# A fused attention and FFN layer: its first stage ordered by one list of all parts, and 30 weight pieces in place of 42 measured in the context's buffer

## The chip, the cores and the metric

The kernel runs on one core of a Trainium2 chip. Its time is the device time of one execution in microseconds (us), the median of several runs. Beside it stands one profiled execution, from which all rows are taken.

## The reference

The input x is (2, 512, 1024). The layer computes

```
n = layernorm(x)
x = x + xattn(n, positions, context)      # context: (2, 1024, 256), used as the weights of a gated MLP
m = layernorm(x)
W = base + mean(|w - base|) * sign(w - base)      # for each of w1, w2, w3 (3584 x 1024)
x = x + (silu(m @ W1.T) * (m @ W3.T)) @ W2.T
```

`xattn` reads the 1024 channels as 256 heads of 4 ways (a small product per head and a normalization), makes q, k and v, turns them by position, takes a causal softmax of 16 heads for each of the 2 batches, and writes the result back into the 1024 channels by a gated update with softplus and exp factors. Then it reads the channels again (two outputs), multiplies them with the context's two matrices, takes silu(gate) * up, and writes back by a second update of the same kind. All is in float32.

For the FFN the mean of |w - base| over a whole matrix must be known before the first weight is used. So each matrix is read once to be measured, 128 rows at a time ("pieces": 28 for each matrix, 84 in all), and later again to be used.

## The kernel before

The work is cut into 8 tiles of 128 rows, 4 for each batch. It has two stages.

The **first stage** does the cross-attention layer and, beside it, the measuring of w1 and w3 (pieces 0 to 55; `SOON` is 56). Its parts have names (stage, number, part):

- `front` (tile, 17 parts): normalization, transposes, the small products with `diag` (the mask product, part 6), q, k and v, their transposes.
- `fill`, `use`, `weigh` (48 units; `fill 36` is unit 36): scores by TensorE into four PSUM banks, then either the maximum (VectorE) or the exponential (ScalarE) as `use`, then the product with v. `turnmax` and `out` belong to groups of units. Units 0 to 24 belong to batch 0, the rest to batch 1 but for unit 23, which begins batch 1. The four banks of scores are shared, so each fill waits for the use of the unit before.
- `row` and `back` (tile): the first write-back, and the read for the MLP. `back` part 20 writes `inT`, the MLP's input.
- `mlp` (32 blocks, 8 for each half batch): 8 matmuls with the context's matrices in `ctxw`, silu, a product.
- `finish` (tile): second write-back, statistics of the new rows.
- `norm` and `turn` (4 tiles each): normalization and transposes for the FFN, in upper and lower parts.
- `measure` (56 pieces): the SP queue loads a piece and its base (512 KB each), VectorE takes the difference (GpSimd for every third piece), ScalarE the absolute sum (`me_abs` counts the pieces done).
- `ctx`: the 2 MB load of the context's matrices into `ctxw`. `coef`: the coefficients from the sums (two small steps of VectorE around a matmul of TensorE). `raw`, `prep`, `upper`, `blend`: the first four weight rows of the FFN, made ready. `early`: the first products of the FFN.

Pieces are measured in buffers that stand in turn (`PARTS` is 3). Pieces whose number is a multiple of 3 use `part`. The two others use `ctxw` as long as their number is below `LATER`, and from then on `big[0]`, the buffer of batch 0's q and k. So `ctx` waits until `LATER` pieces are measured, and the load of piece `LATER` waits for the last weighing of batch 0:

```python
if t == LATER:
    sp.wait_ge(at_pv, TURN[last_unit("T", len(GROUPS) // 2 - 1)] + 1)
```

`phase_one_order()` makes the order of the parts on each engine (TensorE is "PE", VectorE "DVE", ScalarE "ACT", GpSimd "POOL") when the program is built. It goes through time with estimated durations. Of the parts that are ready it takes the one with the lowest `start - LEAD[...]`, the start less a tabulated lead. The engines then work through their lists in this order and wait for each other by semaphores; the durations of the plan have no other effect.

`LULLS` names parts of TensorE ahead of which it multiplies a unit matrix some times (line 1449): "filler". An entry is (count, bank, the user whose readers are waited for first, or None for half-width filler with no wait). It keeps TensorE active where the plan expects a wait.

The **second stage**, `ffn_order()`, has its own lists: the products with w1 and w3, then those with w2. The diff leaves it alone.

Of the kernel before, what the change touches and what calls it, by code (L numbers as in the profile page):

```python
# [152 lines left out]
LATER, SOON = 42, 2 * JT  # L153
# [232 lines left out]
def lead(key):  # L386

    stage, t, part = key
    return LEAD[stage, part][t]


def phase_one_order():
# [58 lines left out]
    while ready:  # L451
        best = None
        for key in sorted(ready):
# [12 lines left out]
            rank = start - lead(key)  # L466
# [50 lines left out]
LEAD = {  # L517
    ("back", 0): (-225.99, -238.77, -359.66, -358.29, -450.97, -468.31, -612.22, -231.01),
    ("back", 1): (6.37, -89.84, -35.64, -348.36, -186, -305.43, -474.36, -667.36),
    ("back", 2): (-228.52, -249.15, -129.37, -360.12, -325.24, -303.49, -528.41, -614.89),  # L520
    ("back", 3): (205.51, -257.89, -88.79, -223.09, -268.08, -203.44, -510.34, -530.38),
    ("back", 4): (-218.43, -230.15, -178.8, -145.66, -451.83, 66.43, -631.77, -586.7),
    ("back", 5): (-223.08, -263.97, -355.17, -282.96, -403.66, -382.05, -485.87, -605.69),
    ("back", 6): (59.69, -290.89, -357.39, -385.03, -474.02, -448.04, -675.86, -616.52),
    ("back", 7): (-236.06, -225.1, -389.92, -48.43, -486.21, -474.98, -393.21, -602.33),
    ("back", 8): (3.19, 30.32, -358.28, -216.22, -486.97, 67.58, -576.98, -587.55),
    ("back", 9): (-281.25, -230.88, -180.3, -381.58, -482.31, -357.42, -625.94, -537.35),
    ("back", 10): (-137.74, -303.66, -410.08, -427.11, -515.73, -517.64, -49.04, -698.31),
    ("back", 11): (-44.49, -119.5, -276.51, -375.63, -232.23, -539.45, -686.78, -416.34),
    ("back", 12): (-301.88, -360.67, -52.9, -232.33, -409.01, -548.28, -591.09, -246.37),  # L530
    ("back", 13): (-43.29, -323.83, -467.45, -499.71, -556.47, -654.5, -112.56, -766.07),
    ("back", 14): (-328.52, -191.13, -479.38, -228.06, -630.23, -354.83, -709.43, -448.81),
    ("back", 15): (5.12, 84.02, -501.87, -542.37, -260.17, -556.77, -826.53, -818.8),
    ("back", 16): (51.96, -375.05, -217.05, -528.19, -473.77, -546.52, -618.88, -737.93),
    ("back", 17): (-338.82, -410.57, -498.3, -444.63, -593.01, -373.83, -463.09, -566.26),
    ("back", 18): (-239.72, -98.17, -407.24, -521.88, -643.69, -697.12, -475.37, -298.36),
    ("back", 19): (-385.54, -423.62, -538.78, -598.71, -633.12, -505.57, -834, -837),
    ("back", 20): (-389.19, -441.08, -439.18, -198.64, -742.05, -462.03, -517.88, -801.02),
    ("blend", 0): (-1059.06, -1156.9),
    ("blend", 1): (-959.72, -721.92),  # L540
    ("blend", 2): (-875.88, -814.02),
    ("blend", 3): (-526.23, -1037.71),
    ("coef", 0): (-305.16,),
    ("coef", 1): (-615.23,),
    ("coef", 2): (-468.02,),
    ("ctx", 0): (-101.35,),
    ("diag", 0): (-56.53, -68.11),
    ("dump", 0): (-636.99, -735.49, -753.18, -747.54, -823.09, -101.99, -907.87, -1049.67),
    ("early", 0): (-922.69, -879.16),
    ("early", 1): (-576.9, -1205.82),  # L550
    ("early", 2): (-720.49, -1030.56),
    ("early", 3): (-1112.76, -1458.21),
    ("fill", 0): (53.95, -90.28, 282.32, -156.82, 31.83, 16.1, -177.4, -184.3, -194.93, -204.96, 50.55, -224.38, -235.42,
# [3 lines left out]
    ("finish", 0): (-283.94, -582.73, -661.89, -707.35, -834.71, -847.17, -919.46, -594.69),  # L557
    ("finish", 1): (-564.04, -588.05, -697.69, -724.73, -714.26, -492.51, -751.68, -914.48),
    ("finish", 2): (-522.27, -519.79, -506.87, -269.19, -632.11, -627.22, -704.37, -832.85),
    ("finish", 3): (-519.56, -488.19, -146.36, -805.7, -639.26, -746.76, -682.15, -891.98),  # L560
    ("finish", 4): (-136.2, -619.53, -610.47, -722.85, -834.27, -876.3, -938.57, -777.13),
    ("finish", 5): (-581.47, -630.04, -454.56, -619.34, -694.69, -863.44, -377.22, -909.27),
    ("finish", 6): (-90.19, 155.1, -723.98, -828.01, -406.89, -492.71, -888.55, -603.59),
    ("finish", 7): (-642.57, -617.83, -431.62, -680.22, -605.76, -793.54, -935.11, -973.45),
    ("finish", 8): (-587.11, -463.8, -503.4, -540.37, -233.96, -647.05, -885.61, -816.41),
    ("finish", 9): (-586.05, -412.71, -574.27, -450.54, -756.17, -793.11, -673.91, -655.59),
    ("finish", 10): (-297.89, -587.86, -639.11, -572.34, -851.43, -626.67, -764.65, -818.29),
    ("finish", 11): (-655.12, -522.12, -778.09, -509.5, -309.29, -806.88, -962.53, -807.86),
    ("finish", 12): (-385.93, -591.05, -838.04, -760.91, -676.85, -649.05, -414.26, -805.06),
    ("finish", 13): (-179.73, -658.06, -841.99, -465.23, -629.34, -894.12, -975.43, -969.75),  # L570
    ("finish", 14): (-721.85, -465.58, -844.37, -477.77, -887.04, -517.18, -874, -766.54),
    ("finish", 15): (-737.68, -743.87, -875.66, -861.7, -859.57, -745.65, -977.29, -781.37),
    ("finish", 16): (-753.16, -293.46, -694.49, -473.82, -935.94, -650.63, -748.65, -538.42),
    ("front", 0): (340.88, -61.51, 92.28, 91.21, -69.31, -82.02, 247.14, -185.56),
    ("front", 1): (182.29, -23, 21.77, -47.12, 162.48, 97.92, -71.75, -68.38),
    ("front", 2): (112.65, -19.03, 290.76, 118.66, 74.76, -86.16, -172.38, -215.67),
    ("front", 3): (-77.36, 18.8, 118.95, -60.39, 356.01, 276.47, 50.59, -254.36),
    ("front", 4): (188.4, 310.84, 55.13, 148.26, 106.28, -11.75, -176.25, 36.87),
    ("front", 5): (481.18, 247.19, 74.37, 76.9, 118.23, 402.54, -4.28, -260.56),
    ("front", 6): (117.35, -67.3, -14.78, 18.98, 162.28, 283.35, -193.47, -293.39),  # L580
    ("front", 7): (88.36, 5.08, 66.5, 63.87, -89.59, -156.74, 214.83, -282.62),
    ("front", 8): (26.63, -68.61, 39.51, 18.86, -84.64, 15.93, -213.04, 94.99),
    ("front", 9): (101.49, 120.16, 261.78, 153.29, -38.03, 89.3, -29.56, -292.97),
    ("front", 10): (624.51, -68.67, -83.91, -81.82, 451.18, -164.66, -34.07, -7.36),
# [2139 lines left out]
```

## Time and profile before

| | us |
|---|---|
| median of 3 runs | 1232.62 (1226.36 to 1236.79) |
| profiled execution, its own time | 1234.41 |
| its span, first to last instruction | 1232.6 |
| TensorE busy | 1181.4 (96%) |
| VectorE busy | 939.4 (76%) |
| ScalarE busy | 703.1 (57%) |
| GpSimd busy | 353.9 (29%) |
| mean granted clock of TensorE | 0.989 |

Read it as shares over two stages that differ: busy times by stretch are what tells them apart. TensorE's busy time holds the filler too. The granted clock is a share of 2.4 GHz; a stretch with 0.75 was half of its time at 1.2 GHz.

### The profile page before, as it was taken

The numbers are of one execution on the slowest core, as the hardware profiler recorded it, in microseconds if no ns is written. First come the engines' busy times: TensorE is split into PE (matmuls) and PEld (weight loads), VectorE is DVE, ScalarE is ACT, GpSimd is POOL, SyncE is SP. The second block draws the span as 40 slices with busy tenths as digits, with TensorE's granted clock in tenths as the row PEclk, the third lists the DMA queues.
The fourth block names the chain that finished last, engine by engine and source line by source line (L and its number), as shares of the span: only waits on it lengthen the run. The fifth ranks groups of instructions, "written<-read, shape, count | busy, mean of one in ns | idle before, by whom it ended". The sixth has DMA issues, their size and how long they took to land. (4 is left out here: it accounts for less than half of the span.)

```text
span 1232.6 us, 17284 instructions
## 1 busy us (share of the span) xinstructions
PE 1181.4 (96%) x6276; PEld 920.6 (75%) x6276; DVE 939.4 (76%) x1279; ACT 703.1 (57%) x1007; POOL 353.9 (29%) x441
## 2 busy tenths in 40 slices
PE   7988889999997999999999999999999999999998
PEld 4765554656775888878888888888788888888887
DVE  6778778778878867787777977778775777888864
ACT  4878667575557666557565666656655333334342
POOL 2233333423522334243553344433340000000000
PEclk8999899999999999999999999999999999999999
DMA  8366678865021257767687676776776968753232
GB/s 353 124 248 246 242 259 303 328 224 199 19 86 51 87 165 254 241 189 242 219 278 237 201 229 211 259 240 189 213 237 222 337 243 277 252 205 120 101 125 99
DMA packets 99065, 257.37 MB, mean 209 GB/s; under 512 B 9363, under 2 KB 23973, under 8 KB 98469
## 3 DMA queue, kind: packets, MB, share of 16 engines
q1 hardware_dynamic: 94948, 241.59, 54.6%
q0 software_dynamic: 4032, 14.68, 6.7%
q8 instruction: 50, 0.82, 0.3%
q14 instruction: 35, 0.28, 0.1%
HBM read 214.81 MB, written 41.42 MB: 208 GB/s over the span
## 5 line engine op out<-in xcount | busy, mean ns | idle before, releaser
L2585 POOL TENSOR_TENSOR raw_w<-raw_w,raw_base 128x256 f32<-128x256 f32 x224 | 197.2, 924 | 184.5 <-DMA raw_base<-in_mean_w 184.3
L2129 ACT ACTIVATE split<-grid 128x1024 fp32r<-128x1024 f32 x98 | 104.0, 1061 | 160.7 <-PE pair L1653 147.7
L2527 DVE TENSOR_TENSOR split<-grid,split 128x1024 fp32r<-128x1024 f32 x98 | 119.7, 1225 | 61.8 <-ACT split L2129 61.6
L1653 PE MATMUL quad<-split 128*128 128x512 f32 x588 | 149.3, 389 | 0.5 <-DVE hid L2534 0.5
L1653 PE MATMUL pair<-split 128*128 128x512 f32 x588 | 149.2, 389 | 0.0
L1653 PEld LDWEIGHTS quad<-split 128*128 128x128 f32 x588 | 110.4, 188 | 23.6 <-DVE split L2527 0.9
L1653 PEld LDWEIGHTS pair<-split 128*128 128x128 f32 x588 | 110.5, 188 | 22.8
L2308 DVE TENSOR_TENSOR ring_lo<-raw_base,ring_hi 128x1024 fp32r<-128x1024 f32 x56 | 70.0, 1251 | 33.1 <-ACT ring_hi L2074 27.1
L1606 PE MATMUL pair<-t_b_hi,ring_hi 128*128 128x512 f32 x224 | 89.0, 397 | 2.8 <-ACT snap L2093 2.7
L1606 PE MATMUL pair<-xnT_hi,ring_hi 128*128 128x512 f32 x224 | 87.4, 390 | 0.7 <-ACT t_b_lo L1981 0.7
L1606 PE MATMUL pair<-t_b_lo,ring_hi 128*128 128x512 f32 x224 | 87.8, 392 | 0.0
L1606 PE MATMUL pair<-xnT_lo,ring_hi 128*128 128x512 f32 x224 | 87.3, 390 | 0.0
L1606 PE MATMUL pair<-xnT_hi,ring_lo 128*128 128x512 f32 x224 | 87.2, 389 | 0.0
L1606 PE MATMUL pair<-t_b_hi,ring_lo 128*128 128x512 f32 x224 | 87.2, 389 | 0.0
L2304 DVE SCALAR_TENSOR_TENSOR raw_w<-quad,coeff,raw_base 128x1024 f32<-128x1024 f32 x52 | 66.5, 1280 | 19.6 <-ACT quad L1923 19.3
L2308 DVE TENSOR_TENSOR ring_lo<-raw_w,ring_hi 128x1024 fp32r<-128x1024 f32 x28 | 40.4, 1445 | 46.1 <-ACT ring_hi L1932 46.1
L1923 ACT ACTIVATE quad<-raw_w 128x1024 f32<-128x1024 f32 x52 | 53.1, 1022 | 26.7 <-POOL raw_w L2585 26.1
L2585 POOL TENSOR_TENSOR ctxw<-ctxw 128x256 f32<-128x256 f32 x56 | 44.1, 817 | 69.8 <-DMA ctxw<-in_mean_w 69.8
L2647 POOL DMA_DIRECT2D late<-in_w x28 | 24.9, 891 | 126.0 <-ACT late L2105 126.0
L2216 DVE TENSOR_REDUCE negwide<-quad 128x4 f32<-128x512 f32 (+3 forms) x32 | 46.9, 1488 | 13.2 <-PE quad L1543 13.1
L1606 PEld LDWEIGHTS pair<-t_b_hi,ring_hi 128*128 128x128 f32 x224 | 42.2, 188 | 13.4 <-ACT snap L2093 5.0
L1864 ACT ACTIVATE prob<-quad 128x1536 f32<-128x1536 f32 (+1 forms) x24 | 38.2, 1590 | 21.2 <-PE quad L1555 12.8
(338 smaller groups left out, 2759.6 us busy)
## 6 DMA issues: line engine op xcount, KB each, us to landing
raw_w<-in_w SPq DMA_DIRECT2D x56, 512.0 KB, 5.7
raw_base<-in_mean_w SPq DMA_DIRECT2D x56, 512.0 KB, 7.4
grid<-h_blocks SPq DMA_DIRECT2D x49, 512.0 KB, 3.7
ctxw<-in_w SPq DMA_DIRECT2D x28, 512.0 KB, 4.3
ctxw<-in_mean_w SPq DMA_DIRECT2D x28, 512.0 KB, 5.7
late<-in_mean_w SPq DMA_DIRECT2D x28, 512.0 KB, 7.5
late<-in_w POOLq DMA_DIRECT2D x28, 512.0 KB, 6.1
grid<-in_mean_w SPq DMA_DIRECT2D x28, 512.0 KB, 4.7
```

The source lines that it names most:

```text
L1606: a = pe.matmul(bank, ww[:, at + k, :], xx, start=first and k == 0 and n == 0, stop=k == half - 1 and n == 2, skip_group_check=not first)
L1653: a = pe.matmul(into[t], found[:, a, t * P:(t + 1) * P], found[:, b, :], start=p == 0 and n == 0 and q < 4, stop=p == PAIRS - 1 and n == 2 ...
L1864: act.activation(probs[TURN[u] % 2][:, :, 0:cols], quad[:, :, 0:cols], ACT.Exp).then_inc(at_p, 1)
L1923: act.activation(spare.rearrange("p a b -> p (a b)"), w[:, :], ACT.Sign).then_inc(f_sign, 1)
L2129: act.activation(splits[n % RINGS][:, 0:2, :], operands(n), ACT.Copy).then_inc(a_hi, 1)
L2216: a = dve.tensor_reduce(found.rearrange("p r j -> p (r j)"), quad[:, :, at:at + cols], AX.X, ALU.max, negate=True)
L2304: dve.scalar_tensor_tensor(w[:, :], sign, coeff[:, k:k + 1], base[:, :], ALU.mult, ALU.add).then_inc(f_w, 1)
L2308: dve.tensor_tensor(whole_of(pair[1]), source, whole_of(pair[0]).bitcast(F32), ALU.subtract).then_inc(done, 1)
L2527: dve.tensor_tensor(found[:, 2:4, :], operands(n), found[:, 0:2, :].bitcast(F32), ALU.subtract).then_inc(a_lo, 1)
L2585: a = pool.tensor_tensor(w[:, some], w[:, some], base[:, some], ALU.subtract)
L2647: pool.dma_start(lates[n % LATES][:, :], d["w2"][n], accum_op=ALU.add).then_inc(ld_add[n % LATES], 16)
```

## The change

The plan's rule is replaced. `LEAD` and `lead(key)` go. A table `RANK` takes their place: each of the 1014 parts has a place of its own, 0 to 1013, and of the ready parts the one with the lowest place is taken. The table came from a search. `LATER` goes from 42 to 30. The `LULLS` table is made anew for the new order. Nothing else is changed.

```diff
-LATER, SOON = 42, 2 * JT
+LATER, SOON = 30, 2 * JT
...
-def lead(key):
-
-    stage, t, part = key
-    return LEAD[stage, part][t]
...
-            rank = start - lead(key)
+            rank = RANK[stage, part][t]
...
-    ("ctx", 0): (-101.35,),
-    ("front", 0): (340.88, -61.51, 92.28, 91.21, -69.31, -82.02, 247.14, -185.56),
+    ("ctx", 0): (396,),
+    ("front", 0): (0, 1, 12, 20, 35, 52, 102, 154),
...
 LULLS = {
     ('front', 0, 4): (14, 0, ('front', 0, 11)),
     ('front', 0, 6): (14, 0, ('front', 0, 11)),
-    ('front', 0, 11): (14, 0, ('front', 0, 11)),
+    ('front', 0, 11): (13, 0, ('front', 0, 11)),
+    ('front', 0, 13): (1, 2, ('front', 0, 13)),
...
-    ('weigh', 24, 0): (8, 4, None),
...
-    ('weigh', 34, 0): (9, 4, ('weigh', 34, 0)),
-    ('fill', 36, 0): (4, 4, None),
-    ('fill', 37, 0): (16, 4, None),
     ('fill', 38, 0): (1, 0, ('fill', 38, 0)),
-    ('weigh', 38, 0): (6, 4, ('weigh', 38, 0)),
```

The whole `LULLS` tables hold 136 filler matmuls before and 78 after. On the lists of TensorE around the context's matrices, the order of the parts is

```
before: ... fill36 fill37 weigh36 back3.12 turnmax13 fill38 weigh38 mlp0 mlp1 mlp2 mlp3 fill39 mlp4 mlp5 mlp6 mlp7 fill40 ...
after:  ... fill36 mlp0 weigh36 fill37 mlp1 mlp2 turnmax13 fill38 mlp3 fill39 mlp4 back3.12 fill40 mlp5 mlp6 mlp7 fill41 ...
```

and at the end of the first stage

```
before: ... mlp31 norm0.1 finish6.0 finish7.0 finish6.2 finish7.2 finish6.4 finish7.4 norm0.3 norm1.1 norm2.1 norm3.1 ... turn0.3 turn0.2 turn1.3 turn1.2 turn0.7 turn1.7 early0.0 ...
after:  ... mlp31 norm0.1 finish6.0 norm1.1 finish6.2 norm0.3 finish6.4 norm2.1 finish7.0 norm1.3 finish7.2 finish7.4 norm3.1 norm2.3 turn0.3 norm3.3 turn0.2 early0.0 ...
```

## Rows read from the trace of the kernel before

**Rows 1.** Busy time by stretch: from:to, length, then each engine's busy us (instructions).

```profile
48.90:205.00 156.10, 139.23 (x1338) 89.56 (x1338) 124.70 (x207) 112.70 (x206) 56.18 (x73) 0.97 0.72 259
205.00:231.00 26.00, 22.14 (x203) 12.26 (x203) 23.16 (x36) 16.39 (x28) 9.77 (x14) 1.00 0.91 331
231.00:329.20 98.20, 92.65 (x590) 64.29 (x591) 75.28 (x135) 57.26 (x111) 41.96 (x58) 0.98 0.51 183
329.20:410.90 81.70, 72.90 (x328) 54.35 (x327) 65.25 (x132) 53.24 (x88) 27.65 (x38) 0.96 0.20 72
0.00:410.90 410.90, 366.32 (x2678) 248.84 (x2679) 322.02 (x610) 268.34 (x478) 145.79 (x205) 0.97 0.56 204
410.90:1232.60 821.70, 815.06 (x3598) 671.75 (x3598) 617.40 (x669) 434.74 (x530) 208.10 (x236) 1.00 0.64 211
```

**Rows 2.** The same stretches, filler matmuls (line 1449) alone.

```profile
48.90:205.00 156.10, 10.44 (x37) 3.48 (x37) 0.97 0.72 259
205.00:231.00 26.00, 7.45 (x39) 3.62 (x39) 1.00 0.91 331
231.00:329.20 98.20, 3.64 (x11) 1.09 (x11) 0.98 0.51 183
329.20:410.90 81.70, 1.53 (x4) 0.39 (x4) 0.96 0.20 72
```

**Rows 3.** Two short stretches with a low granted clock (PEclk).

```profile
134.00:142.00 8.00, 6.78 (x43) 3.82 (x44) 4.97 (x8) 5.17 (x9) 3.32 (x5) 0.57 0.67 248
...
392.00:405.00 13.00, 9.32 (x42) 7.44 (x42) 12.66 (x21) 11.39 (x13) 6.95 (x8) 0.74 0.12 40
```

**Rows 4.** Timeline of the start: start us, us, engine, line, what; VectorE, then TensorE.

```profile
11.34 0.16 DVE L2153 SCALAR_TENSOR_TENSOR stat_ln<-stat_ln 128x1 f32<-128x1 f32 x1 [0.68 <-POOL stat_ln L2579]
...
11.41 1.28 DVE L2145 BATCH_NORM_STATS2 stat_ln<-prob 128x6 f32<-128x512 f32 x2
...
14.66 5.25 PE L1449 MATMUL quad<-unit 128*128 128x512 bf16 x14
...
19.75 1.92 PE L1478 MATMUL pair<-diag,xT 128*128 128x96 f32 x16
```

**Rows 5.** Timeline: input of the cross-attention (ScalarE), context load (SP's queue).

```profile
200.01 1.50 ACT L2027 ACTIVATE inT<-pair,gb 128x128 f32<-128x128 f32 x4
...
221.20 0.33 SPq L1318 DMA_DIRECT2D ctxw<-in_ctx  x1
```

**Rows 6.** Timeline of TensorE ahead of the first mlp block.

```profile
219.75 1.91 PE L1449 MATMUL pair<-unit 128*128 128x256 bf16 x16
...
222.56 0.93 PE L1540 MATMUL quad<-big 32*128 32x384 f32 x8 [0.90 <-ACT prob L1864]
...
230.84 7.17 PE L1709 MATMUL pair<-inT,ctxw 128*128 128x256 f32 x32
```

**Rows 7.** Timeline: last weighing of batch 0 (TensorE), issue of weight piece 30.

```profile
155.38 0.86 PE L1513 MATMUL pair<-prob,vaug 128*32 128x256 f32 x16 [0.44 <-ACT prob L1864]
...
167.17 0.33 SPq L1314 DMA_DIRECT2D part<-in_w  x1
```

**Rows 8.** VectorE: timeline rows, and busy time of the stretch 281.8 to 329.2.

```profile
226.48 1.22 DVE L2422 TENSOR_TENSOR part<-part 128x1024 f32<-128x1024 f32 x1
...
293.21 0.96 DVE L2285 TENSOR_TENSOR hid<-hid,wr_q 128x768 f32<-128x768 f32 x1
...
308.17 1.37 DVE L2285 TENSOR_TENSOR hid<-hid,wr_q 128x768 f32<-128x768 f32 x1
...
281.80:329.20 47.40, 44.67 (x246) 31.77 (x246) 38.66 (x80) 22.73 (x47) 25.31 (x34) 0.96 0.33 123
```

**Rows 9.** Timeline of TensorE at the end of the first stage.

```profile
382.14 5.22 PE L1587 MATMUL pair<-wcat,inner 128*128 128x376 f32 x16
...
393.65 1.34 PE L1729 MATMUL quad<-ident,work 128*128 128x128 f32 x8 [3.05 <-ACT xnT_lo L1955]
...
416.90 0.60 PE L1745 MATMUL pair<-ident,work 128*128 128x128 f32 x4
```

More of the change, by code:

```diff
@@ L871 @@
     ('front', 0, 6): (14, 0, ('front', 0, 11)),
-    ('front', 0, 11): (14, 0, ('front', 0, 11)),
+    ('front', 0, 11): (13, 0, ('front', 0, 11)),
+    ('front', 0, 13): (1, 2, ('front', 0, 13)),
     ('front', 1, 11): (3, 0, ('front', 1, 11)),
-    ('turnmax', 3, 0): (4, 6, ('weigh', 5, 0)),
-    ('row', 0, 0): (1, 6, ('row', 0, 0)),
-    ('fill', 10, 0): (1, 4, ('back', 0, 0)),
-    ('back', 0, 4): (1, 6, ('front', 5, 15)),
+    ('fill', 3, 0): (1, 0, ('fill', 3, 0)),
+    ('turnmax', 3, 0): (1, 6, ('weigh', 3, 0)),
@@ L878 @@
+    ('weigh', 7, 0): (1, 6, ('weigh', 7, 0)),
+    ('row', 0, 0): (1, 7, ('row', 0, 0)),
+    ('turnmax', 5, 0): (2, 7, ('turnmax', 5, 0)),
     ('fill', 14, 0): (1, 0, ('fill', 14, 0)),
-    ('fill', 15, 0): (3, 6, ('weigh', 14, 0)),
-    ('fill', 17, 0): (4, 4, ('front', 6, 13)),
-    ('fill', 21, 0): (2, 4, ('turnmax', 7, 0)),
+    ('fill', 16, 0): (3, 4, ('weigh', 14, 0)),
+    ('fill', 17, 0): (1, 6, ('front', 6, 11)),
+    ('fill', 18, 0): (1, 0, ('fill', 18, 0)),
     ('turnmax', 7, 0): (2, 4, ('turnmax', 7, 0)),
-    ('fill', 22, 0): (1, 0, ('fill', 22, 0)),
@@ L895 @@
-    ('fill', 37, 0): (16, 4, None),
-    ('fill', 38, 0): (1, 0, ('fill', 38, 0)),
-    ('weigh', 38, 0): (6, 4, ('weigh', 38, 0)),
-    ('fill', 41, 0): (2, 4, None),
-    ('fill', 42, 0): (1, 0, ('fill', 42, 0)),
-    ('finish', 0, 4): (1, 6, ('weigh', 42, 0)),
-    ('fill', 46, 0): (1, 0, ('fill', 46, 0)),
-    ('row', 6, 0): (1, 0, ('row', 7, 0)),
-    ('back', 6, 0): (1, 0, ('row', 7, 0)),
-    ('row', 7, 2): (2, 5, ('back', 7, 0)),
-    ('back', 7, 4): (1, 6, ('mlp', 10, 0)),
-    ('finish', 2, 4): (1, 3, ('finish', 3, 0)),
@@ L907 @@
-    ('finish', 4, 2): (1, 4, ('back', 7, 19)),
-    ('finish', 4, 4): (1, 4, ('back', 7, 19)),
-    ('finish', 5, 4): (1, 5, ('mlp', 25, 0)),
-    ('turn', 0, 3): (1, 4, ('turn', 0, 3)),
+    ('fill', 22, 0): (1, 6, ('front', 6, 15)),
+    ('back', 3, 0): (2, 6, ('back', 3, 0)),
+    ('back', 3, 2): (1, 7, ('turnmax', 10, 0)),
+    ('fill', 29, 0): (3, 0, ('fill', 29, 0)),
+    ('row', 4, 0): (1, 6, ('back', 4, 0)),
+    ('row', 4, 2): (4, 6, ('back', 4, 0)),
+    ('back', 4, 2): (1, 4, ('row', 5, 0)),
@@ L911 @@
+    ('fill', 38, 0): (1, 0, ('fill', 38, 0)),
+    ('weigh', 47, 0): (1, 4, ('mlp', 8, 0)),
+    ('back', 6, 0): (1, 2, ('back', 6, 0)),
+    ('finish', 5, 2): (1, 3, ('mlp', 24, 0)),
+    ('finish', 7, 4): (1, 4, ('norm', 3, 1)),
+    ('turn', 1, 7): (1, 2, ('turn', 2, 3)),
 }
```

240 lines of the change are left out of this document (119 added, 121 removed), and 21 rows, old and new, of the table LEAD.

## The prediction

> **What bounds the kernel now.** I read the busy times by stretch first. From 410.9 us on, TensorE is busy for 815.1 of 821.7 us [rows 1]: the second stage (the FFN) runs at TensorE's own pace, and the diff touches nothing of it. So whatever the change does must show as an earlier or later start of that stage. The reader is to look at the stretches before it. There TensorE shows 366.3 of 410.9 us, but part of that is filler: line 1449 multiplies a unit matrix, only to keep the engine active. Taking the filler rows [rows 2] from the busy rows [rows 1], and the busy rows from the lengths, I get after the start-up:
>
> - 48.9 to 205 us: 16.9 idle and 10.4 filler
> - 205 to 231: 3.86 idle and 7.45 filler
> - 231 to 329.2: 5.5 idle and 3.6 filler
> - 329.2 to 410.9: 8.8 idle and 1.5 filler
>
> That is 35 us idle and 23 us filler, 58 us in which TensorE does no work of the reference. No single engine fills the stage: VectorE is busy for 124.7 of 156.1 us in the first of these stretches and 23.2 of 26 in the second [rows 1]. What costs time is the order: who stands in front of whom on four in-order engines. The granted clock adds a bit. In 134 to 142 us it was 0.57, in 392 to 405 us 0.74 [rows 3], that is 2 x 0.43 x 8 = 6.9 us and 2 x 0.26 x 13 = 6.8 us at 1.2 in place of 2.4 GHz. Matmuls take up to twice as long at that level, so each of the two cost at most 3.4 us.
>
> **What the change is, in terms of the trace.** No instruction of the reference's work is added or removed. The new table is a permutation of all 1014 parts (0 to 1013), and it breaks no dependency, so the new order on each engine can be read off it. On TensorE's list the parts move by 1.8 places on average, on VectorE's and ScalarE's by 4, and the filler falls from 136 matmuls to 78. Both tables have 45 at the start. In the four stretches above they go from 37, 39, 11 and 4 (counts in [rows 2]) to 26, 1 or 2, 3 and 3, cutting the list of fillers at the same parts. I go through it by stretches; each term is a shift of the start of the second stage.
>
> **A, start-up, +1.0 us.** VectorE now takes the statistics of tile 1 before the last step of tile 0's normalization. In the trace of before that step (line 2153) ran at 11.34 us and the statistics of tile 1 (1.28 us for the pair, and two small steps) came behind it [rows 4]. They find their data already there, since they began with no wait. In front of it they take 1.28 + 0.21 + 0.15 less overlaps, against the 0.68 us that VectorE idles there now, so tile 0's rows come about 1 us later. The first mask product of tile 0 started at 19.75 us right behind 14 fillers that took 5.25 us [rows 4], not behind its operands, and these 14 start when the transposes of tile 0 are done; so the delay goes through. Bounds: 0 (the clock rises sooner) to +1.5 us.
>
> **B, the context's matrices, -5 us.** LATER falls from 42 to 30: weight pieces 30 to 41 are measured in the key buffer and not in ctxw, so the 2 MB of context matrices can be loaded 12 pieces sooner. The reader is to see three times [rows 5]: the input of the cross-attention's first block is written at 200.01 + 1.50 us, the context load is issued only at 221.20, and its matmuls start at 230.84. In between TensorE has 11.3 us of idle time and filler: 16 fillers from 219.75, then 0.90 us idle behind them [rows 6]. The new list puts block 0 of the mlp between fill 36 and fill 37, blocks 1 and 2 behind fill 37, and block 3 behind fill 38. A block costs 7.17 / 4 = 1.8 us [rows 6], four 7.2 us. Block 0 fits whole where the 16 fillers stand (1.91 + 0.90 us). Blocks 1 and 2 stand in front of a transpose that waited for VectorE, and are longer than that wait, so I count half of them; block 3 fits mostly. That makes 5 us that no longer has to be done behind 231 us. Bounds: 0 (the attention's own chain through ScalarE and VectorE gets longer by what is put in) and -9 us (all four, and row and back parts in place of the 9 fillers ahead of them).
> This adds a wait on SP's queue: piece 30 now waits for the last weighing of batch 0, whose matmuls began at 155.38 us, and behind it in the queue stand the later pieces and the context load. Piece 30 was issued at 167.17 us [rows 7], 12 us later. The new list runs the pieces some 4 ahead at that point, so the wait may bite for a few us; three buffers are in flight and the measuring has slack to the end of the stage, so I cost it at nothing. If that cover were gone, the context load would come later by the same few us; it would still be some 40 us ahead of 221.
>
> **C, the rest of the attention (48.9 to 205 us), -2 us.** Here the same parts are interleaved more evenly; VectorE's load per unit of attention gets flatter. 11 fillers fewer at 10.44 / 37 = 0.28 us each [rows 2] would be 3.1 us if all of it were waiting that has gone. I take 2, as a filler that is left out turns into idle time where the wait stays. Bounds -7 (a quarter of the idle and filler time) and +4 us (one new fall of the clock, and a new wait like the old).
>
> **D, the measuring is postponed, +1 us.** Before, all 56 measured pieces are behind TensorE at the end of the attention (281.8 us). The new list leaves 6 of them for later: 4 subtractions of VectorE at 1.22 us [rows 8], 2 of GpSimd, and 7 passes of ScalarE. They land where VectorE has 38.7 of 47.4 us busy [rows 8], and make that 43.5. TensorE in that stretch is at 44.7, so it stays ahead of VectorE. Bounds 0 and +5. The coefficients move with it (from fill 46 to finish 4 on TensorE), and so do the four preparations of raw weights; they are due at the first product, 410.9 us, so I cost them at nothing. If that cover went, TensorE would stand at its small matmul of the coefficients for a weight piece that is still on its way.
> Beside this a rule of the skill. VectorE's `hid<-hid,wr_q` took 0.96 us at 293.21 and 1.37 us at 308.17, when GpSimd was subtracting raw weights [rows 8]. The Trainium skill (GPSIMD Engine Reference, Specifications) says that GpSimd shares its SBUF interfaces with VectorE and contends with VectorE instructions that have two SBUF inputs. By this rule, with which the trace agrees, the four postponed subtractions would cost up to 0.4 us more each, 1.6 us; that lies inside the upper bound, and the sum goes without it.
>
> **E, the end of the stage, -3 us.** Before, TensorE waited 3.05 us before the transposes of norm 2 [rows 9], with a low clock in the same stretch [rows 3]. The new list spreads the norms between finish 6 and finish 7, and starts the first weight product behind two turns and not four. That covers the 3.05 us and perhaps two thirds of the clock's 3.4 us: up to -5.5 us. Against it, finish 7 now starts about 3.1 us later, behind norm 1, norm 2 and three small parts of finish 6, and its chain through VectorE and ScalarE leads to turn 3, which stood at 416.90 us, 34.8 us behind the start of finish 7 at 382.14 [rows 9]. If that chain is tight, the end moves by +3.1. It had 6 us of first products in front of it, which can be done later; so I take -3.
>
> Other falls of the clock may go or come; I take 0 there.
>
> Sum: +1 - 5 - 2 + 1 - 3 = -8 us. The profiled execution took 1234.4 us for a span of 1232.6, so it would take 1226.4. The median of the runs shown is 1.8 us below it, so **I predict 1224.6 us**.
>
> **Rivals.** *It balances better than I count.* The list of all parts was changed on every engine, so waits fall everywhere, not only where I looked. For it: 58 us of idle and filler time and 58 fillers fewer. Against it: TensorE's own order hardly moves. If a third of the 58 us went in place of B to E (19), with A: -18, 1214.6 us.
>
> *The gain is off the path.* The attention's units hang on each other through TensorE, VectorE and ScalarE in turn. If that loop ends last, work put into the waits only lengthens it, and B and C are 0; with A, D and E: -1, about 1232. It includes the case that the change does nothing that can be seen. For it: fillers were at places where TensorE waited for others, and they cost nothing there.
>
> *Slower: VectorE becomes the bound from 282 to 359 us.* Postponed pieces bring it to 43.5 of 47.4 us, 92%. In 48.9 to 205 us, with VectorE at 80%, TensorE idled 16.9 of 156.1 us, 11% [rows 1]; at that rate the 47.4 us would hold 5.1 idle, at 92% say double that, 10.3, against 2.7 now [rows 8]: +7.6. What is late there stays late in the finishing parts behind it: half as much again, +3.8. A wait can pull the clock down as at 134 us: one such fall, +3.4. With A, and B, C and E at 0: up to +15.8; for the middle of this case I take two thirds, +11, 1243.6 us. It decides from the point at which VectorE has more than about 45 us of work in the 47. The Trainium skill (TensorE: Matmul & The Clock Gate, What's actually happening) states that TensorE is throttled by default and that activity releases it; by that rule fewer fillers speak against the change. The trace agrees that idle time comes before a fall (134 us), and shows falls with the fillers in place.
>
> **How the numbers follow.** Forecast (1219 to 1231) 0.47; better balance 0.20; off the path 0.22; slower 0.11. The range leaves out the lower third of the second case and the upper half of the last, and a little of the bounds: 1212 to 1240 us. 1% is 12.3 us, about what a measurement of this kernel can tell from no change. Below 1220.3 lie most of the second case and the edge of the first, 0.26; above 1244.9 half of the last, 0.06; the rest, 0.68, is within 1%.
>
> **What would show it.** B: the context load issued before 190 us, the first cross-attention matmuls some 10 us sooner, almost no filler around them. E: the first weight product ahead of turn 1, at about 404 us. A: the mask product at about 20.7 us. D: VectorE above 43 us in the 47 us behind the attention, with TensorE's idle time there not doubled. Behind the early products the second stage is alike to within 2 us. I am wrong if that part moves, if TensorE idles in the postponed measuring, or if the clock falls at new places in the attention.

## The result and the profile after

The changed kernel takes 1198.03 us (median of 4 runs, 1197.02 to 1199.19) against 1231.11 us (4 runs of the kernel before beside it). The ratio is 0.9731, interval 0.9701 to 0.9761: 33 us. I had forecast 1224.6 us with a range of 1212 to 1240. The direction was right and the size off by a factor of four.

The profiled execution took 1198.74 us for a span of 1197.0, 35.6 us less than the span of before. I cut both traces at the same four parts: the last weighing of batch 0, the first mlp product, finish 7, and the first product of the second stage that uses its own transposed tile. First the changed kernel, then the one before (from:to, length, busy us of PE, PEld, DVE, ACT, POOL with instructions, granted clock, DMA share, GB/s).

```profile
0.00:151.19 151.19, 132.19 (x1156) 88.86 (x1157) 119.40 (x240) 109.93 (x192) 53.31 (x73) 0.98 0.72 265
151.19:205.64 54.45, 51.17 (x489) 31.28 (x489) 52.51 (x94) 37.19 (x76) 23.89 (x31) 1.00 0.74 272
205.64:358.17 152.53, 147.99 (x892) 106.00 (x890) 132.14 (x241) 114.17 (x198) 72.68 (x90) 1.00 0.48 176
358.17:396.57 38.40, 34.94 (x189) 26.64 (x188) 34.69 (x56) 30.12 (x37) 12.08 (x13) 1.00 0.23 82
...
0.00:396.57 396.57, 366.29 (x2720) 252.78 (x2721) 338.73 (x628) 291.40 (x501) 161.96 (x205) 0.99 0.58 214
396.57:1197.00 800.43, 796.19 (x3498) 656.18 (x3498) 606.15 (x651) 423.04 (x517) 205.95 (x236) 1.00 0.66 216
```

```profile
0.00:155.38 155.38, 134.59 (x1153) 89.67 (x1153) 118.51 (x241) 106.47 (x186) 47.67 (x69) 0.96 0.66 244
155.38:230.84 75.46, 66.02 (x610) 40.37 (x610) 62.85 (x105) 51.20 (x96) 28.51 (x41) 0.98 0.81 292
230.84:382.14 151.30, 143.03 (x813) 102.24 (x810) 115.14 (x218) 90.19 (x170) 58.25 (x81) 0.99 0.40 143
382.14:429.13 46.99, 40.91 (x209) 31.98 (x207) 39.68 (x67) 32.59 (x41) 12.35 (x15) 0.93 0.21 79
...
0.00:429.13 429.13, 384.54 (x2779) 264.26 (x2779) 336.18 (x627) 280.46 (x490) 146.78 (x206) 0.97 0.55 199
429.13:1232.60 803.47, 796.84 (x3499) 656.33 (x3497) 603.24 (x653) 422.62 (x517) 207.11 (x236) 1.00 0.65 214
```

The filler alone, of the changed kernel (line 1415 there) and of the one before (line 1449), over the first stage:

```profile
0.00:396.57 396.57, 25.80 (x78) 0.99 0.58 214
```

```profile
0.00:429.13 429.13, 37.31 (x136) 0.97 0.55 199
```

The reader is to take length minus busy: TensorE idled 44.6 us of the first stage before and 30.3 after, 14.3 us less. Filler fell by 11.5 us. What is left of its busy time (384.54 - 37.31 = 347.2, and 366.29 - 25.80 = 340.5) fell by 6.7 us, though it is the same work. Together that is the 32.6 us by which the second stage starts sooner, as it must be, since the three make up the length. I put the 6.7 us down to the clock, which is argued and not measured by itself. Before, behind the start-up, it fell at four places, two of them [rows 3]; the two others are these. At the four together 3.4 + 3.4 + 1.7 + 1.7 = 10.2 us of clock were not granted, so the 6.7 us find room in them:

```profile
185.00:190.00 5.00, 4.91 (x48) 3.00 (x49) 3.89 (x7) 4.20 (x10) 4.41 (x7) 0.66 0.95 369
311.00:318.00 7.00, 6.12 (x20) 4.11 (x21) 5.26 (x11) 2.97 (x5) 4.09 (x5) 0.76 0.01 2
```

The changed kernel has none of them. Behind the start-up its clock is whole to the end:

```profile
49.00:1197.00 1148.00, 1123.10 (x5999) 881.08 (x5999) 911.49 (x1178) 686.65 (x970) 354.81 (x417) 1.00 0.63 213
```

Two more things stand in the tables. At the weighing TensorE is only 4.2 us ahead, but ScalarE has already done 109.9 against 106.5 us of work and GpSimd 53.3 against 47.7, in less time. These engines have more work behind them than TensorE's lead tells. And VectorE's share of the first stage rose from 78% (336.18 of 429.13) to 85% (338.73 of 396.57), while TensorE waited less.

The rows that answer to [rows 4 to 7] and [rows 9] are, in the changed kernel: the mask product behind its 14 fillers, weight piece 30 and the context load on SP's queue, the last weighing of batch 0, the first mlp product, finish 7, the first weight product, and the wait ahead of the second stage's own products.

```profile
15.46 5.25 PE L1415 MATMUL quad<-unit 128*128 128x512 bf16 x14
20.55 1.92 PE L1444 MATMUL pair<-diag,xT 128*128 128x96 f32 x16
...
151.19 0.86 PE L1479 MATMUL pair<-prob,vaug 128*32 128x256 f32 x16
152.89 0.33 SPq L1280 DMA_DIRECT2D part<-in_w  x1
166.58 0.43 SPq L1284 DMA_DIRECT2D ctxw<-in_ctx  x1
205.64 1.95 PE L1675 MATMUL pair<-inT,ctxw 128*128 128x256 f32 x8
358.17 5.22 PE L1553 MATMUL pair<-wcat,inner 128*128 128x376 f32 x16
370.93 0.47 PE L1572 MATMUL pair<-xnT_hi,ring_hi 128*128 128x512 f32 x1 [0.31 <-ACT xnT_lo L1921]
396.57 0.47 PE L1572 MATMUL pair<-t_t_hi,ring_hi 128*128 128x512 f32 x1 [1.69 <-ACT snap L2050]
```

I add one part ahead of which neither kernel has a product with the context's matrices: fill 36. First before, then after: its first row, the busy times from fill 0 to it, and VectorE's waits for scores (line waited for: us in total, times, longest) in that stretch.

```profile
218.11 0.71 PE L1550 MATMUL quad<-big 32*128 32x256 f32 x8 [0.78 <-DVE negwide L2216]
48.91:218.11 169.20, 150.39 (x1423) 95.34 (x1422) 135.91 (x221) 121.66 (x223) 59.85 (x79) 0.97 0.74 264
DVE negwide L2216 <- PE quad L1543: 11.3, 10, 3.3
...
204.00 0.71 PE L1516 MATMUL quad<-big 32*128 32x256 f32 x8
49.99:204.00 154.01, 141.57 (x1397) 90.54 (x1396) 135.98 (x223) 117.06 (x217) 62.33 (x76) 1.00 0.75 273
DVE negwide L2182 <- PE quad L1509: 3.5, 7, 1.0
```

TensorE leads there by 14.1 us, and by 9.7 at fill 33 (199.90 to 190.19). The two engines had waited for each other in turn: TensorE's idle time in the stretch falls from 18.8 to 12.4 us, VectorE's wait for the scores from 11.3 to 3.5.

The context load went out 54.6 us sooner (221.20 to 166.58) and the first mlp product 25.2 us sooner (230.84 to 205.64). The 16 fillers and the 0.90 us of idle time ahead of it [rows 6] are gone, and so is the 3.05 us wait for the transposes of norm 2 [rows 9]. The second stage itself takes 3.0 us less (803.47 to 800.43), 2.4 of it idle time. That is no more than its own spread: in the profiled executions of the experiments it took 799.4 to 804.0 us (807.5 in one), and 801.8 with the old list.

### The profile page after: what moved, and what is told of

It is laid out like the page before. It is cut to its first block, busy times and chain, and to the rows that moved or that the text cites. A ratio compares the mean times of both kernels' runs of the same rounds, so it can differ in the third digit from the quotient of the medians.

```text
span 1197.0 us, 17179 instructions
## 1 busy us (share of the span) xinstructions
PE 1162.5 (97%) x6218; PEld 909.0 (76%) x6218; DVE 944.9 (79%) x1279; ACT 714.4 (60%) x1017; POOL 367.9 (31%) x441
## 4 chain that ended last, share of the span: by engine, by line
PE 79%; DVE 12%; ACT 5%; issue 3%; DMA 1%; POOL 1%; SPq 0%; ACTq 0%; DVEq 0%
PE pair L1572 30%; PE quad L1572 12%; PE quad L1619 11%; PE pair L1619 11%; DVE negwide L2182 3%; PE pair L1553 2%; PE quad L1516 1%; PE quad L1506 1%; ACT prob L1830 1%; DVE wr_q L2235 1%; PE pair L1479 1%; DVE inner L2370 1%; ACT sgate L2001 1%; PE quad L1553 1%; PE quad L1521 1%
## 5 line engine op out<-in xcount | busy, mean ns | idle before, releaser
L2270 DVE SCALAR_TENSOR_TENSOR raw_w<-quad,coeff,raw_base 128x1024 f32<-128x1024 f32 x52 | 66.5, 1280 | 14.2 <-ACT quad L1889 14.0
L1572 PEld LDWEIGHTS pair<-t_b_lo,ring_hi 128*128 128x128 f32 x224 | 42.0, 188 | 9.9
L1572 PEld LDWEIGHTS pair<-t_b_hi,ring_lo 128*128 128x128 f32 x224 | 42.1, 188 | 9.3
```

Of the source, the lines that this page charges most:

```text
L1572: a = pe.matmul(bank, ww[:, at + k, :], xx, start=first and k == 0 and n == 0, stop=k == half - 1 and n == 2, skip_group_check=not first)
L2270: dve.scalar_tensor_tensor(w[:, :], sign, coeff[:, k:k + 1], base[:, :], ALU.mult, ALU.add).then_inc(f_w, 1)
```

## The experiments

The theory that I formed from these tables is **whole order**: no moved group of parts carries the gain. It says that the searched list lets each engine find its next operand ready a little more often, the small leads pass from engine to engine, and the freed buffer is only a condition for it. The rivals are **context** (the early matrices carry it), **weave** (the measuring stood in the attention's way and is now placed better), and **filler and clock**. Each kernel was timed beside the one before, whose median in the comparisons was 1231.3 to 1233.4 us.

One fact about the two lists guides the reading: cut both after any number of parts, and what one has done and the other has not is at most 22 parts of 1014, mostly 4 to 10. 514 parts move by ten places or less; the coefficients move by 166 (634 to 800) and the context load by 107 (503 to 396).

### The buffer, with the old list and with the new

The first kernel has the old order written out as places, the old filler, and the buffer free from piece 30 on. The second has the new order without that.

```diff
-    ("ctx", 0): (396,),
+    ("ctx", 0): (503,),
...
-    ("front", 0): (0, 1, 12, 20, 35, 52, 102, 154),
+    ("front", 0): (0, 4, 12, 17, 37, 52, 104, 165),
```

> The order of the kernel before, written out as a table of places for all 1014 parts, with its own filler; only LATER is 30 instead of 42, so the context's matrices may be loaded from piece 30 on, but the list leaves their load and all that uses them where they were. Theory 'order': a buffer that is free sooner is worth nothing by itself: 1231, within 2 us of the kernel before. Rival 'buffer': what the pieces 30 to 41 collided with in the old buffer was itself a cost: 1224 or less.

```diff
-LATER, SOON = 30, 2 * JT
+LATER, SOON = 42, 2 * JT
```

> The changed kernel with LATER put back to 42: the context's matrices can only be loaded behind the twelfth-next weight piece, and the planner, which takes the ready part with the lowest place, puts the mlp parts behind that; the rest keeps the new order. Theory 'context': most of the 33 us is work of the second kind (mlp) that fills TensorE's idle time behind the middle of the attention: 1215 to 1225. Rival 'balance': the order of all the other parts carries the gain: 1200 to 1208.

With the old list the buffer is worth nothing: 1231.68 us, ratio 1.0012 (0.9990 to 1.0033). Without the buffer the new list takes 1218.2 us, ratio 0.9895 (0.9866 to 0.9924), 20 us more than with it. TensorE's timeline of this second kernel shows where some of it goes, and SP's queue why:

```profile
219.56 1.91 PE L1406 MATMUL pair<-ident,hid 128*128 128x128 f32 x8
229.22 11.02 PE L1675 MATMUL pair<-inT,ctxw 128*128 128x256 f32 x40 [7.75 <-issue]
```

```profile
220.11 0.33 SPq L1284 DMA_DIRECT2D ctxw<-in_ctx  x1
```

The context load goes out at 220.11 us, TensorE idles 7.75 us for it, and 205 to 231 us had a granted clock of 0.66. Fill 36 starts at 204.27 us in it, 13.8 us sooner than before and as in the changed kernel (204.00), so the lead up to there owes nothing to the buffer. So 13 us of gain need no early context, but the list as it is needs it. The number hit the forecast of the context theory. What it measures, though, is a stall in a list that was made for the other case, not what early mlp work gives.

### Early mlp work and late measuring, moved as groups

Four kernels move a group as a whole, all with the buffer free from piece 30 on. The two with mlp parts moved into the old list have 94 and 96 filler matmuls and not 136: what stood around fills 36 to 38 was left out, and a few found no bank. A moved part stands behind as many parts of the other kind as it does in the list that it comes from. The diffs are against the changed kernel and show one line each of the table. The mlp parts alone in their new places, so that all else differs from the changed kernel:

```diff
-    ("coef", 0): (800,),
+    ("coef", 0): (634,),
```

> The order of the kernel before, with one group moved: the context load and the parts of the mlp products stand where the new order has them, counted by how many other parts stand ahead of each (load at place 405 instead of 503, first product 496 instead of 533, last 863 instead of 878); LATER 30, and the 35 filler matmuls around fill 36 to weigh 38 left out, since mlp work stands there now. Theory 'context': the early mlp work is the cure by itself, 1205 to 1215. Theory 'whole order': VectorE and ScalarE work has to be in place for it, and these engines still have the measuring ahead: 1222 to 1230. Rival 'collision': ScalarE's silu work in the attention delays its exponentials: 1232 or more.

The measuring, raw pieces and coefficients alone:

```diff
-    ("ctx", 0): (396,),
+    ("ctx", 0): (491,),
```

> The order of the kernel before, with the other group moved: the measuring of the 56 weight pieces, the four raw pieces and the coefficients stand where the new order has them (the last piece at place 786 instead of 633), everything else as before, LATER 30. Theory 'postponing': VectorE, which the attention's chains wait for, has more time for them in 100 to 280 us: 1218 to 1226. Theory 'whole order': the measuring is only a filler for VectorE's idle time, and moving it without the rest changes little: 1229 to 1234. Rival 'late coefficients': the second stage's first operations then wait: 1235 or more.

Both:

```diff
-    ("front", 0): (0, 1, 12, 20, 35, 52, 102, 154),
+    ("front", 0): (0, 4, 13, 18, 38, 52, 105, 165),
```

> Both groups moved in the old order (mlp and context load, and measuring), everything else in the old order. If the two groups carry the gain together: 1203 to 1210, near the changed kernel. If their gains only add up from the two single moves: the sum of what the kernels with one group each give. Theory 'whole order': the attention's own parts and those of the finish have to be reordered too, 1218 to 1228.

And the changed kernel with its mlp parts put back:

```diff
-    ("ctx", 0): (396,),
+    ("ctx", 0): (503,),
```

> The changed kernel with the context load and the mlp parts put back to where the old order has them (load at place 503, first product 533, last 878), the rest in the new order, LATER 30. Theory 'context': the kernel loses most of the gain, 1218 to 1228. Theory 'whole order': 1203 to 1212, since early mlp work is worth some 10 us.

They took 1312.3, 1294.1, 1325.0 and 1265.0 us, ratios 1.0648, 1.0501, 1.0753 and 1.0270. That is 37 to 97 us above the highest number of my theories; only the rivals that said "or more" hold two of them. A group set among parts that weren't ordered for it makes waits in many places, and the clock falls with them: the means were 0.961, 0.970, 0.955 and 0.973. These runs say that the lists don't take a group moved by rule. They don't say what a group would be worth in a list made for it, so they decide neither for nor against the context theory, except for the start: in the last of them, with the mlp put back, fill 36 still comes at 203.91 us; only the hope that one group could be given to the old order falls.

### Joins of the two lists

Each join has one list for its first n parts and then what is left in the order of the other. The filler follows the part that it belongs to, in the bank that the joined plan gives (22 matmuls of it find none in the join at 447, 4 in the reverse join at 340). The edit is in the table alone, as in the join at 340:

```diff
-    ("front", 0): (0, 1, 12, 20, 35, 52, 102, 154),
+    ("front", 0): (0, 4, 12, 17, 37, 52, 104, 165),
```

First the ones that begin with the old list:

> The old order for its first 340 parts (to the 26th of the 48 score products, 155 us; the sets of parts done by then differ by 4 between the two orders), then the new order; LATER 30. Theory 'adds up along the list': what is lost is the 4.8 us by which the changed kernel is ahead there, 1198 + 5 = 1203. Rival 'early part makes the later one possible': 1210 or more. The seam itself may cost a little, with the reverse join the two show how much.

> The old order for its first 458 of 1014 parts (to just ahead of the score product fill 33, some 200 us), then the rest in the new order with LATER 30. If the gain adds up along the list as the starts of the score products show it (9.7 us in hand at fill 33 of the changed kernel), 1198 + 10 = 1208. If the early gain is only room that a later bound takes back: 1198 to 1202. If the early order is what makes the later one possible (the mlp can't start sooner without it): 1218 or more.

> The old order for its first 750 parts (some 320 us, half of the mlp products; the sets differ by 8), then the new order. Theory 'adds up': the changed kernel is 26 to 27 us ahead there, so 1198 + 26.5 = 1224.5. If the two orders' ends differ by more than that (as the seam at place 878 showed: 50 us above the changed kernel), the seam or the old order's first 750 parts leave VectorE behind: 1232 or more.

> The old order for its first 878 parts (up to the last mlp product, 375 us), then the new order of the end of the first stage and of the second. By the starts in the two traces the changed kernel is 26.1 us ahead at the last mlp product and 32.6 us ahead at the first product of the second stage: so 1231 minus some 6.5 (end of the first stage) = 1224.5, and a stall or two less in the second stage at 3 us, 1222. If the end's order only pays because work came in sooner: 1229 to 1232.

Then the reverse:

> The reverse join: the new order for its first 340 parts, then the old one with its own filler; LATER 30. Theory 'adds up': 1231.5 - 5 = 1226.5. Rival 'the early lead is lost again at a later wait, unless the later order uses it': 1230 to 1232. A seam that costs: over 1232. Together with the join the other way round: the two sum to 1198 + 1231.5 = 2429.5 if no seam costs anything.

> The new order for its first 447 parts (up to ahead of fill 33, 190 us), the old order behind it, with its own filler as far as its banks allow; LATER 30. The join at place 340 gave 1223.7. If the gain adds up by the starts on TensorE (9.7 us of lead at fill 33) plus what VectorE is ahead: 1231.5 - 15 = 1216. If the stretch 340 to 447 gives nothing of its own: 1223 or so. Rival 'seam': over 1226.

> The new order for its first 750 parts (some 300 us, half of the mlp products), the old order for the end of the first stage. By the starts on TensorE all but some 6 us of the lead is in hand there: 1198 + 6 = 1204. If the end of the stage carries as much as the join at place 878 made it look: 1215 or more. If the end's order is worth nothing: 1198 to 1200.

| first n parts | old first: us, ratio, interval | new first: us, ratio, interval | sum of ratios less 1.9731 |
|---|---|---|---|
| 340 | 1210.78, 0.9815 (0.9778 to 0.9852) | 1223.70, 0.9914 (0.9886 to 0.9941) | -0.0002, 0 us |
| 458 and 447 | 1214.29, 0.9864 (0.9839 to 0.9888) | 1239.31, 1.0062 (1.0030 to 1.0093) | 0.0195, 24 us |
| 750 | 1238.69, 1.0033 (1.0013 to 1.0053) | 1219.80, 0.9906 (0.9876 to 0.9936) | 0.0208, 26 us |
| 878 | 1248.01, 1.0141 (1.0110 to 1.0172) | not run | |

Few of the forecasts above held. The joins at 340 missed 'adds up' (1203 and 1226.5 forecast), the first by 8 us, which put it into its rival's range of 1210 or more, the second by 3 to the good side. At 458, 1214.29 lies between all the ranges. At 878 the time is 16 us above the highest number. At 447 and at 750 (both ways) it was the rival with a cost at the seam or at the end that held.

The last column is a test of a join. If the seam cost nothing, the two ratios would sum to those of both kernels, 0.9731 + 1. At 340 they do, within the 7 us that the three intervals leave: the first 340 parts (155 us) would be worth (0.9815 - 0.9731) x 1232 = 10.3 us by the one and 0.0086 x 1232 = 10.6 us by the other, to some 6 and 3 us. But the sum can agree though a seam costs. In the join with the old list first, VectorE and then TensorE wait behind the seam for a weight piece that is still on its way:

```profile
160.98 1.23 DVE L2387 TENSOR_TENSOR part<-part 128x1024 f32<-128x1024 f32 x1 [6.63 <-DMA part<-in_mean_w]
165.52 0.44 PE L1535 MATMUL pair<-ident,o_sb 128*128 128x128 f32 x2 [4.39 <-DVE o_sb L2199]
```

So a part of its 10.3 us is this stall, and the clock was low for 3.4 us behind it. TensorE's lead at that point is 4.2 us in the changed kernel. In the join with the new list first the lead over the kernel before is 5.5 us at fill 26 and 7.3 at the first own product of the second stage (421.80), and the rest of its gain lies in the second stage. So 4 to 10 us are what the runs show for the first 340 parts.

Behind that the seams cost 24 and 26 us by the sums, as much as what is to be shared out (at 447 the 22 missing fillers may be a part of it). Two can be read in detail. In the join at 878, TensorE and VectorE:

```profile
373.27 1.04 PE L1709 MATMUL quad<-ident,work 128*128 128x128 f32 x8
382.66 1.00 PE L1567 MATMUL quad<-wcat,inner 128*128 128x376 f32 x1 [8.36 <-DVE inner L2384]
```

```profile
374.86 1.27 DVE L2284 SCALAR_TENSOR_TENSOR raw_w<-raw_w,coeff,raw_base 128x1024 f32<-128x1024 f32 x1
376.88 2.48 DVE L2284 SCALAR_TENSOR_TENSOR raw_w<-raw_w,coeff,raw_base 128x1024 f32<-128x1024 f32 x2 [0.76 <-ACT raw_w L1898]
...
382.18 0.42 DVE L2384 TENSOR_TENSOR inner<-quad,sgate 128x256 f32<-128x256 f32 x1 [2.08 <-ACT sgate L2015]
```

The new list has the preparation of raw weights on VectorE sooner than the old one. Set behind the old head it comes ahead of the last `inner`, 0.42 us of work, and finish 6 waits 8.36 us for that. In the join at 750 with the new list first, the old place of the coefficients meets the postponed measuring, and the clock falls behind the wait:

```profile
307.47 0.56 PE L1686 MATMUL quad<-csum,ones 128*128 128x2 f32 x2 [5.86 <-issue]
```

```profile
307.00:320.00 13.00, 12.53 (x54) 11.06 (x55) 7.62 (x20) 5.55 (x13) 6.75 (x10) 0.71 0.15 42
```

One join has no wait of TensorE above 2 us behind its seam, the one at 458 with the old list first. Its starts of fill 33 and of the first own product are

```profile
200.66 0.93 PE L1506 MATMUL quad<-big 32*128 32x384 f32 x8
410.44 0.47 PE L1572 MATMUL pair<-t_t_hi,ring_hi 128*128 128x512 f32 x1 [1.70 <-ACT snap L2050]
```

It is 0.8 us behind the kernel before at the first and 18.7 ahead at the second. So the new list from there on brings 19.5 us on the old head too, where the changed kernel gains 22.9 (9.7 to 32.6). By these starts the head and the rest divide: some 10 us up to fill 33, some 20 behind it. The time of this join, 16 us above the changed kernel's, says that a few us are lost between the two. Between middle and end the joins don't divide them, for there each tail meets other engines that aren't where it expects them. That is what the whole-order theory says, and it is shown for the seams; that the gain behind fill 36 spreads over many parts is argued from it.

### The measuring made tiny

```diff
-                    dve.tensor_tensor(w, w, base, ALU.subtract).then_inc(me_dve, 1)
+                    dve.tensor_tensor(w[:, 0:64], w[:, 0:64], base[:, 0:64], ALU.subtract).then_inc(me_dve, 1)
```

and the same for GpSimd's subtraction and ScalarE's sum, in both orders.

> The order of the kernel before, LATER 30, with the measuring of the 56 weight pieces made tiny: difference and sum of magnitudes over 64 instead of 1024 columns on VectorE, GpSimd and ScalarE (leaves out most of the measuring, so the coefficients are others); loads and order stay. It takes some 44 us of VectorE and 54 us of ScalarE out of the first stage. Theory 'weave' (the measuring stands in the way of the attention's chains in the old order, and the new order places it better): much faster, 1195 to 1210, and within 12 us of the new order with the same cut. Theory 'whole order': 1212 to 1225, and still 20 us or more above the new order with the same cut.

> The changed kernel with the same cut: measuring over 64 columns (leaves out most of the measuring). Its VectorE is at 19 of 20 us in several stretches, so time taken from it should show: theory 'weave', 1188 to 1195, the gap to the old order under 12 us. Theory 'whole order': 1180 to 1192 with the gap 20 us or more. Rival 'TensorE bounds it already': 1194 to 1198, nothing gained.

Old order 1225.22 us, ratio 0.9942 (0.9921 to 0.9962); new order 1194.85, ratio 0.9693 (0.9662 to 0.9725). The first stage of the new one over the same length as before:

```profile
0.00:396.57 396.57, 369.04 (x2747) 256.69 (x2748) 300.72 (x634) 251.71 (x507) 107.18 (x155) 1.00 0.58 215
```

VectorE has 38 us less to do in it, ScalarE 40 and GpSimd 55, and the kernel gains 3 to 5 us, with intervals that overlap (0.9693 against 0.9731). The old order gains 7. By its number alone the new one missed the whole-order forecast (1180 to 1192) and hit the rival's (1194 to 1198, nothing gained). What decides is the gap between the orders: it stays at 0.0249 x 1232.5 = 30.7 of 33 us, where weave wanted under 12. The weave theory falls as far as the measuring's busy time goes, and with it the thought that VectorE's load bounds the stage: that load is worth 3 to 7 us in either order. The loads of the pieces stayed in these runs, so waits for them aren't tested. The traces bound them: from fill 0 to fill 36 VectorE waits for pieces for 4.2 us before and some 2 after, and ScalarE for the differences that VectorE and GpSimd make for 7.2 and 5.3.

### Filler

Both kernels lose all filler but the 42 matmuls ahead of tile 0's parts, that is 94 and 36 matmuls (91 and 33 of them behind 49 us). The old order has LATER 30 too:

```diff
-    ('turnmax', 3, 0): (1, 6, ('weigh', 3, 0)),
-    ('weigh', 7, 0): (1, 6, ('weigh', 7, 0)),
...
-    ('turn', 1, 7): (1, 2, ('turn', 2, 3)),
```

> The order of the kernel before with its filler matmuls behind the start-up left out (94 of 136, 22 of 37 us of TensorE), LATER 30. Theory 'filler only stands in gaps': it costs nothing and, where it kept the clock up, its loss costs: 1232 to 1245. Rival 'filler is in the way of the work behind it': 1222 to 1228. With the changed kernel having only 33 behind its start-up, this bounds what the filler has to do with the 33 us.

> The changed kernel without its 36 filler matmuls behind the start-up. In the old order the like cost 6 to 8 us, with a granted clock of 0.982 over the run. Theory 'filler is only needed where there are gaps': 1197 to 1201, clock 0.995 or more. Rival 'the clock stays up because of filler here too': 1204 or more with the clock under 0.99.

Old order: 1239.56 us, ratio 1.0047 (1.0020 to 1.0074), 6 us more. New order: 1204.85, ratio 0.9770 (0.9734 to 0.9805) against 0.9731, some 5 to 7 us more, at the edge of what the intervals tell apart. The first is what the theory forecast; the second has the time of its rival but not its clock, 0.994. Filler isn't in the way in either, so its smaller number is a sign of fewer waits, not a source of the gain. In the new order a fall of the clock comes back, here:

```profile
155.00:205.00 50.00, 44.41 (x402) 26.65 (x404) 45.66 (x78) 32.22 (x69) 22.17 (x28) 0.93 0.68 258
```

But the first stage is hardly longer for it: the first own product stands at 397.11 us in that profiled execution, against 396.57. The other 7.1 us lie in the second stage (807.50 against 800.43), which has no filler in either kernel; there TensorE waits 5.1 us for `snap` at three places, and the clock falls once more. So no price of filler in the new order is shown beyond a us or two, and why the second stage was longer stays open.

### The start-up

```diff
-    ("front", 0): (0, 1, 12, 20, 35, 52, 102, 154),
+    ("front", 0): (0, 4, 12, 20, 35, 52, 102, 154),
```

> The changed kernel with the first eight parts in the old order (statistics of tile 0 not behind those of tile 1, mask product on TensorE some 0.8 us sooner); both orders have done the same parts by then. By the starts of the score products the lead of the old start is gone by the third of them: 1198, within 1 us. If the start still counts: 1197. If it costs: 1200.

1197.00 us, ratio 0.9709 (0.9679 to 0.9739), against 0.9731 (0.9701 to 0.9761). The two can't be told apart; the start is worth nothing to 3 us. The number is the one forecast for a start that still counts, but it lies inside the noise. No version that does all of the work was faster by more than that.

## Why the prediction was wrong

**The step that failed is term C**, and the reason by which I held the rival "it balances better than I count" at 0.20: "TensorE's own order hardly moves". That is true of the list and says nothing of the time. TensorE waits for operands, and when they come is set by the order on the other engines; on VectorE and ScalarE the parts move by 4 places on average. I had allowed C 2 us, at most 7. TensorE's lead was 4.2 us at the last weighing of batch 0, 9.7 at fill 33, where C's stretch ends, and 14.1 at fill 36, with no product of the context's matrices done. The kernels with the new list and the buffer late, or with the mlp put back, show the same lead there (13.8 and 14.2), so it belongs to the order of the attention's own parts, which is C.

- **The bound.** Right: the second stage runs at TensorE's pace, the gain is an earlier start of it (32.6 of 35.6 us of the span). The 58 us of idle time and filler was the right pool, but I drew 8 us from it. With the start-up it gave 25.8, and the rest of TensorE's busy time 6.7 on top, the clock's part, for which I had taken 0 outside of E.
- **A, +1.0.** The delay came (mask product at 20.55, forecast 20.7) and was gone by the third score product, which starts within 0.1 us of before. Undone, the start is worth nothing that can be told.
- **B, -5.** Its signs came: load before 190 us, 2 fillers around the first blocks. The first mlp product was to come 10 us sooner and came 25.2 sooner. The piece 30 was issued 1.7 us behind the start of the weighing that it waits for, so that wait was covered for the queue. The buffer by itself is worth 0. I had costed B as four blocks put into waits at one place; the runs tell that the buffer is a condition (20 us are lost without it in this list), not a term that can be added. From fill 36 to the last score product, where B had to show, the lead grows from 14.1 to 23.8 us, 9.7 where I had 5 and a bound of 9; how much of that is the mlp work and how much the order of the rest no run tells.
- **D, +1.** No cost seen. From the last score product to the 17th mlp block VectorE had 39.55 of 44.4 us, 89% (forecast above 43 of 47, 91%), and TensorE idled 2.4 us:

```profile
258.00:302.40 44.40, 41.96 (x239) 30.18 (x240) 39.55 (x80) 30.97 (x63) 19.62 (x25) 1.00 0.40 143
```

  The rival of a VectorE bound falls with the thin runs: taking the work of the measuring away gives 3 to 7 us in all.
- **E, -3.** Right in mechanism, small in size. The lead grew from 26.1 us at the last mlp product to 32.6 at the first own product of the second stage: 6.5 us, over my bound of 5.5 (whose two terms, 3.05 and two thirds of 3.4, sum to 5.3). The first weight product stands ahead of turn 1, as said.
- **Second stage.** Forecast alike to 2 us; it took 3.0 less, which its spread between executions covers.
- **Off the path** (0.22): falls. **Fewer fillers speak against the change**: the Trainium skill (TensorE: Matmul & The Clock Gate, What's actually happening) has TensorE throttled unless activity releases it. The clock stayed whole with 58 fillers fewer, and TensorE idled less too, 30.3 against 44.6 us; with the rest of the filler taken out as well it fell to 0.93 in one stretch, and in the old order to 0.982 over the run. Rule and runs agree, and the conclusion I drew from the rule was wrong.

What stays open is how the 18.5 us behind fill 36 divide between earlier mlp work and better order of all else. Groups and joins both cost more in waits than what they were to tell apart.

## What to carry to other kernels

When a whole order is replaced, don't add up the few spots where the lists visibly differ: take the pool of idle time, filler and low clock over the stage, and ask how much of it no single engine's load explains. Here 26 of the 82 us of idle time and filler in the first stage went, and 7 us of low clock. An order is one object: a piece of a good one set on a piece of another was up to 50 us worse than the good one and up to 17 worse than the bad one, and a moved group up to 93 worse. Read the lead at parts that both orders have done: it showed 14 of the 33 us before any of the visible change could act. And test a cut both ways, for where the two joins don't sum to the two kernels no share of a part is a number; where they do, look in the trace for a stall at the seam all the same.

## What was not expected of the hardware

With VectorE, ScalarE and GpSimd relieved of 38, 40 and 55 us of work in one stage of 397 us, the time fell by 3 to 7 us only: VectorE, busy for 85% of that stage, and ScalarE, for 73%, set the pace here by the order of their operands, not by their load. In the groups moved as a whole, waits of 4 to 14 us brought the clock down with them, to a mean of 0.955 over 1325 us: 0.045 x 1325 = 60 us not granted, where the kernel before has 0.011 x 1233 = 14. That is up to 46 of the 93 us lost, less what fell on idle time.
